# High and low parts of two weight matrices stored interleaved by element, and the SBUF buffers laid out anew

## The chip, the cores and the metric

One core of one Trainium2 chip. The metric is the device time of one launch in microseconds; the number for the kernel before is 1211.54 us, the median of three runs (1210.9 to 1212.32). Engines are named as in the profile: PE is TensorE's matmul side, PEld its weight loads, DVE is VectorE, ACT is ScalarE, POOL is GpSimd, SP is SyncE.

## The reference

A layer of linear attention followed by a gated feed-forward part, gated once more by a ternary product. x is 8 x 2048 x 256 in float32.

```python
xn = layernorm(x)
q, k, v = split(xn @ Wqkv + bqkv)              # 256 -> 3 x 256
qp, kp = elu(q) + 1, elu(k) + 1
kv = einsum('bsd,bse->bde', kp, v)
attn = (qp @ kv) / (qp . sum_s(kp) + 1e-6)
z = layernorm(xn + attn) * g1 + b1
ffn = (silu(z @ Wg + bg) * (z @ Wu + bu)) @ Wd + bd     # 256 -> 682 -> 256
s = layernorm(z + ffn) * g2 + b2
g = silu(xn @ ternary(weight).T * scale)
out = x + s * g
```

## The kernel before, in words

The 16384 rows are worked in 32 groups (`GROUPS`) of 512 rows (`TOK`, four tiles of 128); four groups make one batch. Every exact product is made of three products of rounded parts: `parts3` pairs high with high, low with high and high with low, where the high part is a rounded copy (`f32r`) and the low part the rest. In `products` (L1271) each pair is one weight load (PEld) and one matmul (PE). The left of a pair is the stationary operand, which the weight load brings into the array (128 columns); the right is the moving operand, streamed past it. The load of the next product's stationary operand starts a few ns after the matmul of the present one and runs beside it.

The jobs of TensorE, written out by hand in `TENSOR_JOBS`, are for each group:

- G 0 to 4, U 0 to 4 and GU 5 (`gate_or_up`): 11 jobs of 6 products, stationary a 128 column slice of `wgu_h` or `wgu_l`, moving `zT_h` or `zT_l`, 512 columns. 2112 products in all.
- Q 0 and 1: 6 products each, stationary `wq_h` or `wq_l`, moving `xT_h` or `xT_l`, 512 columns. 384 products.
- D 0 to 5 (`Dn`): stationary `h_h` or `h_l`, moving `wd_h` or `wd_l`, 256 columns; 12 products for each of D 0 to 4, 4 for D 5. 2048 products.
- K, B, XK, KV and N: products with 256 or 258 moving columns, stationary `xT`, `xn`, `kv` (as `xk`) and `qp`.

The steady order of the jobs is

```python
TENSOR_JOBS = steps("""
    K 0, D 4, KV 0, KV 1, D 5, K 1, N 0, N 1, N 2, N 3, G 0, U 0, G 1, U 1, G 2, B 0, U 2, Q 0, Q 1,
    B 1, G 3, D 0, D 1, U 3, G 4, XK 0, U 4, XK 1, XK 2, XK 3, GU 5, D 2, TZ 0, TZ 1, D 3""")
```

so of the eleven gate-up jobs six come right behind a job with 256 or 258 moving columns: G 0 (behind N 3), U 2 (behind B 0), G 3 (behind B 1), U 3 (behind D 1), U 4 (behind XK 0) and GU 5 (behind XK 3). The other five follow a gate-up job.

The weights are split into high and low once, in the fill: `gu_high` (L695 for ACT) writes `wgu_h[:, c, :]`, `setup_gu_low` (L1226 on DVE) writes `wgu_l[:, c, :]`; `setup_q_high` and `setup_qk_low` (L1184) do the same for the query weights. Nothing writes them later.

SBUF buffers are laid out in the order in which `build_kernel` declares them, each at the next multiple of 32 bytes in every partition. All slices of the stationary and moving operands that the six products of a job use are a multiple of 256 bytes from their buffer's start (except for the second half of `qp` and `kv`, which are 32 bytes further), so a buffer's start modulo 256 holds for each of its products:

| buffers | role | before | after |
|---|---|---|---|
| `wgu_h`, `wgu_l` | stationary of G, U, GU | 96 | 224 (high), 228 (low) |
| `zT_h`, `zT_l` | moving of G, U, GU | 96 | 96 |
| `wq_h`, `wq_l` | stationary of Q | 96 | 32 (high), 36 (low) |
| `xT_h`, `xT_l` | moving of Q, stationary of K, B | 96 | 96 |
| `h_h`, `h_l` / `wd_h`, `wd_l` | stationary / moving of D | 96 / 32 | 96 / 32 |
| `wk`, `tern` | moving of K, B | 64 | 64 |
| `xn_h`, `xn_l` / `kp_h`, `kp_l` | stationary / moving of XK | 96 / 0 | 96 / 0 |
| `qp` / `kv` | stationary / moving of N | 96 / 32 | 96 / 32 |
| `wv_h`, `wv_l` | moving of KV | 96 | 224 |
| `xa`, `xn`, `kp`, `xq`, `rz`, `sg`, `hs` | operands of DVE, ACT, POOL and the DMAs | 192 | 224 |

Of the kernel before, what the change touches and what calls it, by code (L numbers as in the profile page):

```python
# [30 lines left out]
P = 128  # L31
D = 256
DC = D // P
H = 682
HF = H // P
HT = H - HF * P
HC = HF + 1
# [6 lines left out]
TOK = 512  # L44
TILES = TOK // P
# [6 lines left out]
SHIFT = 8  # L52
# [9 lines left out]
LN0 = LEAD + 1  # L62
# [150 lines left out]
def build_kernel(nc, x, wqkv, bqkv, wg, bg, wu, bu, wd, bd, g1, b1, g2, b2, wt, out):  # L213
    f32, f32r = mybir.dt.float32, mybir.dt.float32r
# [9 lines left out]
    with ctx:  # L224
        def sb(name, shape, dt=f32):
            return ctx.enter_context(nc.sbuf_tensor(name, shape, dt))
# [2 lines left out]
            return ctx.enter_context(nc.semaphore(name))  # L229


        ident = sb("ident", [P, P])
        consts = sb("consts", [P, 4])
        masks = sb("masks", [P, 2])
        norm1 = sb("norm1", [P, 2, TILES])
        norm2 = sb("norm2", [P, 2, TILES])
        kp_h = sb("kp_h", [P, TILES, D], f32r)
        kp_l = sb("kp_l", [P, TILES, D], f32r)
        den = sb("den", [P, 2, 2])
        wd_h = sb("wd_h", [P, HC, D], f32r)  # L240
        wd_l = sb("wd_l", [P, HF, D], f32r)
        kv_h = sb("kv_h", [P, DC, D + SHIFT], f32r)
        hb = sb("hb", [P, 2 * HC])
        hb0 = sb("hb0", [P, 2 * HC])
        hb1 = sb("hb1", [P, 2 * HC])
        kv_l = sb("kv_l", [P, DC, D + SHIFT], f32r)
        ve = sb("ve", [P, 3, TILES])
        vecs = sb("vecs", [P, 5, DC])
        rstd0 = sb("rstd0", [P, LN0, TILES])
        wk_h = sb("wk_h", [P, DC, D], f32r)  # L250
        wk_l = sb("wk_l", [P, DC, D], f32r)
        tern = sb("tern", [P, DC, D], f32r)
        tscale = sb("tscale", [P, 4])
        wq_h = sb("wq_h", [P, DC, D], f32r)
        wq_l = sb("wq_l", [P, DC, D], f32r)
        xT_h = sb("xT_h", [P, XT, DC, TOK], f32r)
        xT_l = sb("xT_l", [P, XT, DC, TOK], f32r)
        h_h = sb("h_h", [P, HRING, TOK], f32r)
# [3 lines left out]
        zT_l = sb("zT_l", [P, DC, TOK], f32r)  # L262
        xn_h = sb("xn_h", [P, TILES, D], f32r)
        xn_l = sb("xn_l", [P, TILES, D], f32r)
        wv_h = sb("wv_h", [P, DC, D], f32r)
        wv_l = sb("wv_l", [P, DC, D], f32r)
        NGU = (2 * HF + 1) * P
        wgu_h = sb("wgu_h", [P, DC, NGU], f32r)
        wgu_l = sb("wgu_l", [P, DC, NGU], f32r)
        qp_h = sb("qp_h", [P, DC, TOK + SHIFT], f32r)  # L270
        nmr0 = sb("nmr0", [P, LN0, TILES])
        mv = sb("mv", [P, 3, TILES, 2])
        qp_l = sb("qp_l", [P, DC, TOK + SHIFT], f32r)
        st = sb("st", [P, 3, TILES, 6])
        bvb = sb("bvb", [P, D])
        bk1b = sb("bk1b", [P, D])
        g1b = sb("g1b", [P, D])
# [10 lines left out]
        sg = sb("sg", [P, SG, TILES, D])  # L288
        hs = sb("hs", [P, 2, TOK])
        ones, one_zero, neg_half = consts[:, 0:1], consts[:, 1:3], consts[:, 3:4]  # L290
        bq, bq1, nbq, g1c, b1c = (vecs[:, n, :] for n in range(5))
        less_h, less_w = masks[:, 0:1], masks[:, 1:2]
        rstd1, nmr1 = norm1[:, 0, :], norm1[:, 1, :]
# [85 lines left out]

        bias_line = xq[:, 1:3, :, :].rearrange("p a t d -> p (a t d)")[0:1, 0:NGU]  # L380
        b1w = nc.dram_tensor("b1w", (NGU,), f32, kind="Internal").ap()
        turned = nc.dram_tensor("turned", (2, D, TOK), f32, kind="Internal").ap()
        z_turned = nc.dram_tensor("z_turned", (2, D, TOK), f32, kind="Internal").ap()
        ROW_PARTS = [slice(at, min(at + 512, NGU)) for at in range(0, NGU, 512)]

# [3 lines left out]
        xk_h, xk_l = kv_h[:, :, 0:D], kv_l[:, :, 0:D]  # L389
        raw_v = xq[:, 1:3, :, :].rearrange("p a t d -> p (a t d)")[:, NGU:NGU + DC * D].rearrange("p (c n) -> p c n", c=DC)  # L390

# [1088 lines left out]
```

## Time and profile before

| | |
|---|---|
| median of three runs | 1211.54 us (1210.9 to 1212.32) |
| profiled execution, its own time | 1212.66 us |
| its span, first to last instruction | 1211.0 us |
| PE busy | 1190.9 us, 98% |
| PEld busy | 1070.2 us, 88% |
| DVE busy | 1082.2 us, 89% |
| ACT busy | 953.3 us, 79% |
| POOL busy | 841.7 us, 70% |
| mean granted TensorE clock | 0.998 of full speed |

The profiled execution's own time is 1.7 us above its span and 1.1 us above the median of the three runs. A matmul's duration in the rows is longer than its turn on the engine: successive matmuls overlap, since the next one enters while the last one drains. The time from one matmul's start to the next one's start is what each costs; the durations differ from it by a constant.

### The profile page before, as it was taken

How to read it: one execution, taken by the hardware profiler on the slowest of the kernel's cores; microseconds unless marked ns; L12 is line 12 of the kernel's file. 1: busy time of each engine (PE TensorE's matmuls, PEld its weight loads, DVE VectorE, ACT ScalarE, POOL GpSimd, SP SyncE). 2: the span in 40 equal slices, each digit the busy share in tenths (PEclk: the TensorE clock that was granted, in tenths of full speed). 3: DMA queues.
4: the chain of work that ended last, by engine and by line, in shares of the span. 5: the costliest groups of instructions: out<-in, count | busy, mean ns of one | idle time of the engine just before them, and what ended most of it. 6: DMA issues, size and time to landing. Idle time of an engine off the chain costs nothing.

```text
span 1211.0 us, 24021 instructions
## 1 busy us (share of the span) xinstructions
PE 1190.9 (98%) x7550; PEld 1070.2 (88%) x7550; DVE 1082.2 (89%) x2467; ACT 953.3 (79%) x1557; POOL 841.7 (70%) x994
## 2 busy tenths in 40 slices
PE   8999999999999999999999999999999999999997
PEld 6889998989988999989999988999988899888886
DVE  6988999999999999999999999999999999777765
ACT  7787888878888887888878888778797788867753
POOL 3443787767787776787767777667776677766676
PEclk9999999999999999999999999999999999999999
DMA  7213432334432334432234432234332343222201
GB/s 217 74 50 88 123 106 70 88 105 123 123 104 72 87 106 123 118 103 78 87 106 122 121 104 74 74 120 123 108 96 63 101 123 105 70 71 61 76 22 35
DMA packets 137524, 115.61 MB, mean 95 GB/s; under 512 B 12340, under 2 KB 122294, under 8 KB 137399
## 3 DMA queue, kind: packets, MB, share of 16 engines
q1 hardware_dynamic: 137398, 114.08, 32.2%
q8 instruction: 62, 1.02, 0.3%
q14 instruction: 64, 0.52, 0.1%
HBM read 67.38 MB, written 46.67 MB: 94 GB/s over the span
## 4 chain that ended last, share of the span: by engine, by line
PE 86%; DVE 7%; issue 2%; ACT 2%; DMA 1%; POOL 1%; SPq 0%; DVEq 0%; POOLq 0%; ACTq 0%
PE bank L1271 61%; PE d_bank L1271 17%; PE xk_bank L1271 7%; DVE st L922 1%; DMA z_turned<-xa 1%; DMA xa<-z_turned 1%; DVE rz L1054 1%; PE bank L1285 1%; DVE bank L1095 0%; DVE h_l L1105 0%; ACT rz L695 0%; DVE zT_l L1085 0%; POOL norm L569 0%; ACT hs L695 0%; DVE kp L1014 0%
## 5 line engine op out<-in xcount | busy, mean ns | idle before, releaser
L1271 PE MATMUL bank<-zT_h,wgu_h 128*128 128x512 f32 x704 | 275.6, 391 | 1.1 <-DVE rz L1054 1.0
L1271 PE MATMUL bank<-zT_l,wgu_h 128*128 128x512 f32 x704 | 275.7, 392 | 0.0
L1271 PE MATMUL bank<-zT_h,wgu_l 128*128 128x512 f32 x704 | 275.4, 391 | 0.0
L695 ACT ACTIVATE rz<-rz,norm 128x256 f32<-128x256 f32 x252 | 140.5, 596 | 57.7 <-DVE norm L1131 57.1
L569 POOL TENSOR_TENSOR norm<-ve,consts 128x4 f32<-128x4 f32 x64 | 72.9, 1139 | 153.6 <-DVE ve L933 153.5
L1271 PE MATMUL d_bank<-wd_h,h_h 128*128 128x256 f32 x640 | 179.2, 280 | 0.1
L1271 PE MATMUL d_bank<-wd_h,h_l 128*128 128x256 f32 x640 | 179.0, 280 | 0.0
L1271 PE MATMUL d_bank<-wd_l,h_h 128*128 128x256 f32 x640 | 179.0, 280 | 0.0
L1095 DVE SCALAR_TENSOR_TENSOR bank<-bank,hb,hs 128x512 f32<-128x512 f32 x160 | 117.9, 754 | 54.0 <-ACT hs L695 42.3
L695 ACT ACTIVATE h_h<-bank 128x512 fp32r<-128x512 f32 x160 | 95.8, 599 | 80.9 <-DVE bank L1095 80.5
L1271 PEld LDWEIGHTS bank<-zT_l,wgu_h 128*128 128x128 f32 x704 | 132.1, 188 | 28.8
L1271 PEld LDWEIGHTS bank<-zT_h,wgu_h 128*128 128x128 f32 x704 | 132.7, 189 | 25.8 <-DVE rz L1054 3.3
L695 ACT ACT_TABLE_LOAD x116 | 148.8, 1283 | 4.1 <-POOL wd_l L678 1.2
L1271 PEld LDWEIGHTS bank<-zT_h,wgu_l 128*128 128x128 f32 x704 | 132.2, 188 | 20.6
L695 ACT ACTIVATE hs<-bank,hb 128x512 f32<-128x512 f32 x192 | 128.3, 685 | 15.0 <-PE bank L1271 13.6
L592 POOL TENSOR_TENSOR ksum<-ksum,kp 128x256 f32<-128x256 f32 x120 | 106.9, 891 | 46.7 <-DVE kp L1021 43.3
L1105 DVE TENSOR_TENSOR h_l<-bank,h_h 128x512 fp32r<-128x512 f32 x160 | 110.0, 688 | 23.1 <-ACT h_h L695 17.4
L1271 PEld LDWEIGHTS d_bank<-wd_h,h_h 128*128 128x128 f32 x640 | 120.2, 188 | 3.1 <-DVE h_l L1105 0.5
L1271 PEld LDWEIGHTS d_bank<-wd_h,h_l 128*128 128x128 f32 x640 | 120.2, 188 | 2.7
L1271 PEld LDWEIGHTS d_bank<-wd_l,h_h 128*128 128x128 f32 x640 | 122.0, 191 | 0.0
L642 POOL TENSOR_TENSOR rz<-rz,g1b 128x256 f32<-128x256 f32 x128 | 118.0, 932 | 0.0
L602 POOL TENSOR_TENSOR rz<-rz,g2b 128x256 f32<-128x256 f32 x124 | 90.4, 739 | 35.0 <-ACT rz L695 35.0
(163 smaller groups left out, 3576.3 us busy)
## 6 DMA issues: line engine op xcount, KB each, us to landing
xq<-in_L_attn_x_dram SPq DMA_DIRECT2D x32, 512.0 KB, 6.0
xa<-in_L_attn_x_dram SPq DMA_DIRECT2D x31, 512.0 KB, 3.9
out_dram<-rz SPq DMA_DIRECT2D x31, 512.0 KB, 5.0
z_turned<-xa SPq DMA_DIRECT2D x120, 128.0 KB, 3.3
xa<-z_turned SPq DMA_DIRECT2D x30, 512.0 KB, 4.1
turned<-xa SPq DMA_DIRECT2D x108, 128.0 KB, 2.5
xa<-turned SPq DMA_DIRECT2D x27, 512.0 KB, 3.9
rz<-in_L_attn_Wg_dram SPq DMA_DIRECT2D x1, 640.0 KB, 5.2
```

What stands on the lines that cost most here:

```text
L569: eng.tensor_tensor(dst, ve[:, k, :], neg_half[:, 0:1].to_broadcast([P, TILES]), ALU.pow).then_inc(S[f"rs{k}"], 1)
L592: eng.tensor_tensor(ksum[:, slot, :], ksum[:, slot, :], part, ALU.add).then_inc(S["ks"], 1)
L602: eng.tensor_tensor(row_, row_, g2b[:, :], ALU.mult).then_inc(S["a"], 1)
L642: eng.tensor_tensor(row_, row_, g1b[:, :], ALU.mult).then_inc(S["zg"], 1)
L695: return eng.activation(out_, in_, func, **kw).then_inc(S[name], 1)
L922: eng.bn_stats(st[:, k, t, :], rows).then_inc(S[f"bn{k}"], 1)
L1054: eng.scalar_tensor_tensor(out=rz[:, g % RZ, t, :], in0=num[:, 0:D], scalar=den[:, n % 2, 1:2], in1=rz[:, g % RZ, t, :], op0=ALU.mult, op1 ...
L1095: eng.scalar_tensor_tensor(out=hidden(g, c)[0:rows, :], in0=up, scalar=hb[0:rows, HC + c:HC + c + 1], in1=hs[0:rows, n % 2, :], op0=ALU.ad ...
L1105: eng.tensor_tensor(h_l[:, slot, :], hidden(g, c)[:, :], h_h[:, slot, :].bitcast(f32), ALU.subtract).then_inc(S["hl"], 1)
L1271: ins = eng.matmul(dst, left, right, start=first and n == 0, stop=last and n == len(pairs) - 1, **kw)
L1285: ins = eng.transpose(dst[:, c * D + t * P:c * D + (t + 1) * P], src[:, 2 * p + t, c * P:(c + 1) * P], ident[:, :])
```

## The change

The high and the low part of the gate-up weights become one buffer `wgu` with the parts side by side: element n of the high part is followed by element n of the low part, so that a slice of 128 columns of either part is read with a step of 8 bytes, over 1024 bytes instead of 512. The same for the query weights (`wq`). The names `wgu_h`, `wgu_l`, `wq_h` and `wq_l` remain as views, so all code that uses them is unchanged. The declarations are put in another order, with one spare buffer of 32 bytes, which gives the starts in the column "after" of the table above. No instruction is added, removed or moved on any engine. In a trace the four views have the names `wgu` and `wq`, and lines behind the declarations stand one further down.

```diff
-        ident = sb("ident", [P, P])
+        NGU = (2 * HF + 1) * P
+        rstd0 = sb("rstd0", [P, LN0, TILES])
+        wgu = sb("wgu", [P, DC, NGU, 2], f32r)
         consts = sb("consts", [P, 4])
...
-        wq_h = sb("wq_h", [P, DC, D], f32r)
-        wq_l = sb("wq_l", [P, DC, D], f32r)
+        norm2 = sb("norm2", [P, 2, TILES])
...
+        spare0 = sb("spare0", [P, 8])
+        ident = sb("ident", [P, P])
         wv_h = sb("wv_h", [P, DC, D], f32r)
         wv_l = sb("wv_l", [P, DC, D], f32r)
-        NGU = (2 * HF + 1) * P
-        wgu_h = sb("wgu_h", [P, DC, NGU], f32r)
-        wgu_l = sb("wgu_l", [P, DC, NGU], f32r)
...
         ones, one_zero, neg_half = consts[:, 0:1], consts[:, 1:3], consts[:, 3:4]
+        wgu_h, wgu_l = wgu[:, :, :, 0], wgu[:, :, :, 1]
+        wq_h, wq_l = wq[:, :, :, 0], wq[:, :, :, 1]
```

where `wq = sb("wq", [P, DC, D, 2], f32r)` now stands between `wd_l` and `norm1`.

## Rows read from the trace of the kernel before

**Rows 1.** The page, part 1: busy time of each engine, share of the span, instructions.
```profile
PE 1190.9 (98%) x7550; PEld 1070.2 (88%) x7550; DVE 1082.2 (89%) x2467; ACT 953.3 (79%) x1557; POOL 841.7 (70%) x994
```
**Rows 2.** Groups of PE, shapes apart: busy us, mean ns; idle before, releaser.
```profile
L1271 PE MATMUL bank<-zT_l,wgu_h 128*128 128x512 f32 x704 | 275.7, 392 | 0.0
L1271 PE MATMUL bank<-zT_h,wgu_h 128*128 128x512 f32 x704 | 275.6, 391 | 1.1 <-DVE rz L1054 1.0
L1271 PE MATMUL bank<-zT_h,wgu_l 128*128 128x512 f32 x704 | 275.4, 391 | 0.0
L1271 PE MATMUL d_bank<-wd_h,h_h 128*128 128x256 f32 x640 | 179.2, 280 | 0.1
...
L1271 PE MATMUL bank<-xT_h,wq_h 128*128 128x512 f32 x128 | 51.5, 402 | 0.0
L1271 PE MATMUL bank<-xT_h,wq_l 128*128 128x512 f32 x128 | 50.1, 391 | 0.0
L1271 PE MATMUL bank<-xT_l,wq_h 128*128 128x512 f32 x128 | 50.0, 391 | 0.0
```
**Rows 3.** Timeline of PE, 18 gate-up products in a row, first and last: start, duration us.
```profile
627.61 0.39 PE L1271 MATMUL bank<-zT_h,wgu_h 128*128 128x512 f32 x1
...
631.69 0.28 PE L1271 MATMUL bank<-tern,xT_h 128*128 128x256 f32 x1
```
**Rows 4.** Tile wgu_h, 627.6 to 631.4 us: duration ns min/median/max.
```profile
L1271 PE MATMUL bank<-zT_h,wgu_h x6: 389/389/389, 627.6 to 631.0; 128*128 128x512 f32 x6
```
**Rows 5.** Tile wgu_h, 600.0 to 601.1 us, right behind a B job.
```profile
L1271 PE MATMUL bank<-zT_l,wgu_h x2: 397/397/397, 600.3 to 601.0; 128*128 128x512 f32 x2
```
**Rows 6.** Tile wgu_h, 607.4 to 608.7 us, right behind an XK job.
```profile
L1271 PE MATMUL bank<-zT_h,wgu_h x2: 393/395/397, 607.4 to 608.1; 128*128 128x512 f32 x2
```
**Rows 7.** Timeline of PE, three query products around a wait.
```profile
635.18 0.39 PE L1271 MATMUL bank<-xT_l,wq_h 128*128 128x512 f32 x1
635.49 0.50 PE L1271 MATMUL bank<-xT_h,wq_h 128*128 128x512 f32 x1
635.83 0.39 PE L1271 MATMUL bank<-xT_h,wq_l 128*128 128x512 f32 x1
```
**Rows 8.** Timeline of PEld in the same stretch.
```profile
634.96 0.19 PEld L1271 LDWEIGHTS bank<-xT_l,wq_h 128*128 128x128 f32 x1
635.49 0.19 PEld L1271 LDWEIGHTS bank<-xT_h,wq_h 128*128 128x128 f32 x1 [0.34 <-DVE h_l L1105]
635.60 0.19 PEld L1271 LDWEIGHTS bank<-xT_h,wq_l 128*128 128x128 f32 x1
```
**Rows 9.** Tile wd_h, 602.0 to 603.9 us and 612.4 to 615.0 us.
```profile
L1271 PE MATMUL d_bank<-wd_h,h_h x6: 276/276/276, 601.9 to 603.6; 128*128 128x256 f32 x6
L1271 PE MATMUL d_bank<-wd_h,h_h x8: 281/281/281, 612.3 to 614.8; 128*128 128x256 f32 x8
```
**Rows 10.** Timeline of PE, D 2 and D 3 (24 products) and their neighbours.
```profile
612.09 0.39 PE L1271 MATMUL bank<-zT_l,wgu_h 128*128 128x512 f32 x1
612.32 0.28 PE L1271 MATMUL d_bank<-wd_h,h_h 128*128 128x256 f32 x1
...
615.15 0.28 PE L1271 MATMUL bank<-wk_h,xT_h 128*128 128x256 f32 x1
```
**Rows 11.** Tiles wgu_h and wgu_l: the writes in the fill, and the readers.
```profile
L695 ACT ACTIVATE wgu_h<-rz,vecs x2: 1452/1454/1455, 26.1 to 29.2; 128x1408 fp32r<-128x1408 f32 x2
L1226 DVE SCALAR_TENSOR_TENSOR wgu_l<-rz,vecs,wgu_h x2: 1679/1681/1683, 27.6 to 33.7; 128x1408 fp32r<-128x1408 f32 x2
L1271 PE MATMUL bank<-zT_h,wgu_l x704: 387/389/398, 78.1 to 1197.8; 128*128 128x512 f32 x176
```

More of the change, by code:

```diff
@@ L229, in sem @@
             return ctx.enter_context(nc.semaphore(name))
-        ident = sb("ident", [P, P])
+        NGU = (2 * HF + 1) * P
+        rstd0 = sb("rstd0", [P, LN0, TILES])
+        wgu = sb("wgu", [P, DC, NGU, 2], f32r)
         consts = sb("consts", [P, 4])
-        masks = sb("masks", [P, 2])
-        norm1 = sb("norm1", [P, 2, TILES])
-        norm2 = sb("norm2", [P, 2, TILES])
         kp_h = sb("kp_h", [P, TILES, D], f32r)
         kp_l = sb("kp_l", [P, TILES, D], f32r)
-        den = sb("den", [P, 2, 2])
+        masks = sb("masks", [P, 2])
         wd_h = sb("wd_h", [P, HC, D], f32r)
         wd_l = sb("wd_l", [P, HF, D], f32r)
[L242 to L249, printed above, removed]
+        wq = sb("wq", [P, DC, D, 2], f32r)
+        norm1 = sb("norm1", [P, 2, TILES])
         wk_h = sb("wk_h", [P, DC, D], f32r)
@@ L252, in build_kernel @@
         tern = sb("tern", [P, DC, D], f32r)
-        tscale = sb("tscale", [P, 4])
-        wq_h = sb("wq_h", [P, DC, D], f32r)
-        wq_l = sb("wq_l", [P, DC, D], f32r)
+        norm2 = sb("norm2", [P, 2, TILES])
         xT_h = sb("xT_h", [P, XT, DC, TOK], f32r)
@@ L264, in build_kernel @@
         xn_l = sb("xn_l", [P, TILES, D], f32r)
+        qp_h = sb("qp_h", [P, DC, TOK + SHIFT], f32r)
+        den = sb("den", [P, 2, 2])
+        nmr0 = sb("nmr0", [P, LN0, TILES])
+        kv_l = sb("kv_l", [P, DC, D + SHIFT], f32r)
+        qp_l = sb("qp_l", [P, DC, TOK + SHIFT], f32r)
+        hb = sb("hb", [P, 2 * HC])
+        hb0 = sb("hb0", [P, 2 * HC])
+        kv_h = sb("kv_h", [P, DC, D + SHIFT], f32r)
+        hb1 = sb("hb1", [P, 2 * HC])
+        ve = sb("ve", [P, 3, TILES])
+        vecs = sb("vecs", [P, 5, DC])
+        tscale = sb("tscale", [P, 4])
+        mv = sb("mv", [P, 3, TILES, 2])
+        st = sb("st", [P, 3, TILES, 6])
+        spare0 = sb("spare0", [P, 8])
+        ident = sb("ident", [P, P])
         wv_h = sb("wv_h", [P, DC, D], f32r)
         wv_l = sb("wv_l", [P, DC, D], f32r)
-        NGU = (2 * HF + 1) * P
-        wgu_h = sb("wgu_h", [P, DC, NGU], f32r)
-        wgu_l = sb("wgu_l", [P, DC, NGU], f32r)
[L270 to L274, printed above, removed]
         bvb = sb("bvb", [P, D])
```

## The prediction

> **What bounds the kernel now.** The page's first part comes first: PE is busy for 98% of the span, no other engine for over 89% [rows 1]. So the time is the sum of what TensorE's 7550 products take, and only two things can move it: the time from one product's start to the next one's, or a wait of PE. The change moves no instruction, so I look at the products themselves.
>
> The groups of PE show which products the change touches [rows 2]: 2112 gate-up products, whose three rows add up to 275.7 + 275.6 + 275.4 = 826.7 us or 391.4 ns each, and 384 query products, 51.5 + 50.1 + 50.0 = 151.6 us. A duration is not a price, since products overlap. The timeline gives the price: 18 gate-up products in a row start from 627.61 to 631.69 us, 226.7 ns apart [rows 3], and in that stretch each has a duration of 389 ns, minimum, median and maximum [rows 4]. So 389 ns of duration stand for 226.7 ns of time, and each ns above it is a ns of time. Behind a B job the same product has 397 ns [rows 5], behind an XK job 393 to 397 ns [rows 6]. Same instruction, same shape, same granted clock (0.998 over the whole span), nothing waits: what differs is how the weight load beside it falls in time against the moving stream. I read the surplus as the two reads of SBUF by TensorE getting in each other's way, and call 389 ns the clean state.
>
> Is 389 ns itself a state with collisions? The query product at 635.18 us has no load beside it: the one before began at 634.96 and the next at 635.49, behind a wait [rows 8]. It too has 0.39 us [rows 7]. So the clean state is the floor of the moving stream, with nothing in it for a new layout of the weights. The same rows price a load: where product and load start together, the next load follows after 635.60 - 635.49 = 0.11 us, and the product's duration is 0.50 instead of 0.39 us. A load with 128 columns occupies its side for about 110 ns: half of a 512 column product's 226.7 ns, but nearly all of a 256 column product's turn.
>
> D shows what a bad phase costs there: its products have 276 ns at 602 to 604 us and 281 ns at 612 to 615 us [rows 9]; 24 of the latter take 615.15 - 612.32 = 2.83 us, 117.9 ns each [rows 10]. The good stretch came behind gate-up products of 397 ns [rows 5], the bad one behind clean ones. The states hang together: what a job inherits decides how it runs.
>
> **The change, part by part.**
>
> *Gate-up.* The load of 128 columns now steps by 8 bytes and goes over 1024 bytes. If it keeps its rate (110 ns), its address moves by 1024 / 110 = 9.3 bytes per ns; the moving stream's by 2048 / 226.7 = 9.0. Before, the load went at 4.7, so the stream overtook it, and whether they met on the way hung on the phase. Now they go almost in step, and the distance at the start (128 bytes modulo 256) stays: over a whole load it drifts by (9.3 - 9.0) x 110 = 33 bytes. If what collides is set by the address modulo 256, or by a smaller power of two that 128 is not a multiple of, they never meet, whatever the phase. Then all gate-up products are clean: 826.7 - 2112 x 0.389 = 5.1 us gone. The ends: nothing gained (0), and at worst all products in the worst state of the rows, 397 ns: 2112 x 0.397 - 826.7 = +11.8 us. I take -5.1, since the two rates match so well and the distance is the largest there is.
>
> *Query.* Of 151.6 - 384 x 0.389 = 2.2 us surplus, 128 x (402 - 389) = 1.7 us belong to each job's first product, which starts together with its load behind a wait [rows 2, 7]; a layout doesn't touch that. I take the rest, -0.5 us. The distance is only 64 bytes; at worst 384 x (397 - 391) = +2.3 us.
>
> *What D inherits.* The clean stretches of D stood behind dirty gate-up products. With clean ones throughout, D 0 and D 1 lose them: all 1920 products at 281 ns are 539.5 us against 179.2 x 3 = 537.6 us (the three D groups are alike, one is shown) [rows 2, 9]: +1.9 us. The other end is that D comes out clean instead, 1920 x (280 - 276) = -7.7 us; nothing in the rows makes that likely, since the loads and operands of D keep their distance of 64 bytes. I take +1.9 us. K, B, XK and N keep all distances, too; I cost them at nothing.
>
> *The fill.* ACT writes the high part in 2 x 1.45 us and DVE the low part in 2 x 1.68 us [rows 11], now with a step of 8 bytes. No row shows an 8-byte step, so the price lies between nothing and twice: at most 2 x 1.68 = +3.4 us, if the two DVE writes doubled and all of it were on PE's path. ACT's write works off 128 x 1408 elements at 1.03 ns each, with its operand from SBUF; I take 0, because G 0, the first reader, comes at 78 us, long behind the last write at 33.7 us [rows 11], and what is delayed in between are single steps beside PE's own queue.
>
> *The other buffers.* Operands of DVE, ACT, POOL and the DMAs shift from 192 to 224 modulo 256. PE has 98%; none of these engines is waited for enough to matter, so 0.
>
> **Sum:** -5.1 - 0.5 + 1.9 = -3.7 us. Against the profiled execution's 1212.66 us that is 1208.96 us; this execution stood 1.1 us above the median of 1211.54 us, so the median should come out at 1207.8 us, 0.3% less. A measurement of this kernel can tell about 0.2% (2.4 us) from no change, so the forecast is just beyond that.
>
> **The rivals.**
>
> *Nothing happens.* The surplus of the dirty states has another cause, or is made elsewhere as fast as it is removed (D at 281 ns is one such place). For it: the gain that can be had is small, 5.6 us, and a phase decides it, not an address that the rows vary; only D's +1.9 us is needed once more to fall under 0.2%. Time: 1211.5 us, from 1209.2 to 1213.9. The Trainium skill, "TensorE: Matmul & The Clock Gate", Part 2, and "SBUF — State Buffer", "Who interferes with whom", say that the weight load has a read port of its own, so that loading the next weights takes nothing from the running matmul. By that rule there is nothing to gain and the change is worth 0; the trace speaks against it in that one product has 389 or 397 ns with nothing but a load beside it.
>
> *In step, and colliding (slower).* What makes the two reads meet never also makes them meet always, if the phase at the start adds the missing bytes: the load starts a few ns behind its matmul, and a few ns are some tens of bytes at 9 bytes per ns. If what counts is the address modulo 128 or 64, a distance of 128 or 64 is none. Also, a load now touches twice as many lines of whatever width. Place: every gate-up and query product. Price: with products at 395 ns on average, the middle of the dirty rows [rows 6], 2112 x (395 - 391.4) = +7.6 us: 1219.1 us. It decides from about 392.5 ns on, where 2.4 us are lost.
>
> *The load becomes slower with its step (slower, more).* A gate-up job's first load runs beside a product with 256 columns, which gives it only some 118 ns [rows 10]. Six jobs per group stand so, 6 x 32 = 192. A load of 1.5 x 110 = 165 ns adds 47 ns each, +9.0 us: 1220.6 us; of twice the time +102 ns each, +19.6 us: 1231.1 us. No row shows a load with a step. The Trainium skill, "SBUF — State Buffer", "SBUF cachelines", wants at least two hits in a line of 16 bytes for full bandwidth; a step of 8 bytes gives just two, so by that page this rival falls. No row here shows it.
>
> *The floor falls.* Were the 226.7 ns themselves collisions, 2496 products could gain. The Trainium skill, "TensorE: Matmul & The Clock Gate", Part 1, gives 215.7 ns between matmuls with 512 columns; by it, up to 11 x 2496 = 27.5 us would go. From the rows alone: 512 columns at the granted 2.4 GHz take 213.3 ns, 13.4 ns less than 226.7, so at most 33 us. Against it stands the product with no load beside it and the same 0.39 us [rows 7, 8].
>
> **How the numbers follow.** Forecast (gate-up clean, D worse or as before): 0.49. Nothing happens: 0.25. In step and colliding: 0.16. Slower load: 0.07. Floor falls: 0.03. Nearly all of the forecast is faster by over 0.2%, a little of it is not, and the floor adds its share: faster 0.50. Same 0.26, slower 0.24. The forecast's own range is 1205.0 (both gains, D as before: -5.6, and 0.9 for jobs that come out cleaner) to 1209.2. The range asked to hold the time 8 times in 10 goes on over "nothing happens" to the colliding case's middle: 1205.0 to 1218.0. It leaves out the slower load, the floor and the upper half of the colliding case.
>
> **What would show it.** In the profile after: the gate-up groups at 389 ns mean instead of 391 and 392, with 389 also behind XK and B jobs (right), or at 393 and more everywhere (the colliding rival). The 18 products between N 3 and B 0 still 226.7 ns apart (floor), and the D groups at 281 (my +1.9) or below 280 (wrong, in the kernel's favour). A slower load shows as a PEld mean above 188 ns and as a longer gap in front of U 2, G 3, U 3, U 4 and GU 5. ACT L695 and DVE L1227 on `wgu` above 1.45 and 1.68 us show a price in the fill. Wrong altogether would be a change in K, XK, N or B, whose operands keep their distances.

## The result, and the profile after

The changed kernel takes 1216.0 us (median of 5 runs, 1215.22 to 1217.15) against 1212.06 us (median of 5) for the kernel before: ratio 1.0036, 95% interval 1.0023 to 1.005. It is slower by 4.4 us by the ratio (the two medians are 3.9 us apart), where 1207.8 us, a gain of 3.7 us, was forecast. The time lies in the range (1205.0 to 1218.0), on the side of the rival "in step, and colliding": it does so because the range reached over to that rival, not by the forecast's own mechanism.

Busy time by engine, changed kernel, answering to [rows 1]:

```profile
PE 1196.2 (98%) x7550; PEld 1089.6 (90%) x7550; DVE 1080.9 (89%) x2467; ACT 953.6 (78%) x1557; POOL 842.4 (69%) x994
```

TensorE has all of it: PE +5.3 us and the weight loads +19.4 us, while DVE has 1.3 us less and ACT and POOL stay within 0.7 us. Groups of PE and PEld, shapes apart, changed kernel (busy us, mean ns), answering to [rows 2]; the first group's busy time is that of products which overlap, so only its mean is of use:

```profile
L1272 PE MATMUL bank<-zT_h,wgu 128*128 128x512 f32 x1408 | 440.9, 394 | 0.8 <-DVE rz L1055 0.8
L1272 PE MATMUL bank<-zT_l,wgu 128*128 128x512 f32 x704 | 277.0, 393 | 0.0
L1272 PE MATMUL d_bank<-wd_h,h_h 128*128 128x256 f32 x640 | 179.1, 280 | 0.0
...
L1272 PE MATMUL bank<-xT_l,wq 128*128 128x512 f32 x128 | 50.4, 394 | 0.0
...
L1272 PEld LDWEIGHTS bank<-zT_h,wgu 128*128 128x128 f32 x1408 | 261.0, 196 | 39.5 <-DVE rz L1055 2.3
```

The gate-up products have 393 to 394 ns instead of 391.4. Their loads have 196 ns; the kernel before has

```profile
L1271 PEld LDWEIGHTS bank<-zT_h,wgu_h 128*128 128x128 f32 x704 | 132.7, 189 | 25.8 <-DVE rz L1054 3.3
```

and 188 ns for the two other groups. D is where it was. In the stretch between N 3 and B 0, where the kernel before was clean, the timeline of PE now reads (x2: two products merged):

```profile
629.99 0.62 PE L1272 MATMUL bank<-zT_h,wgu 128*128 128x512 f32 x2
...
634.61 0.39 PE L1272 MATMUL bank<-zT_l,wgu 128*128 128x512 f32 x1
634.85 0.28 PE L1272 MATMUL bank<-tern,xT_h 128*128 128x256 f32 x1
```

and the tile's durations there

```profile
L1272 PE MATMUL bank<-zT_h,wgu x14: 391/393/397, 629.5 to 634.2; 128*128 128x512 f32 x14
```

21 products from 629.99 to 634.85 us are 231.4 ns each, against 226.7 ns [rows 3] and 389/389/389 [rows 4]. Not one product of this stretch is clean. Compare that with the forecast: all clean. Over the whole trace, 63% of the gate-up products have a duration of at most 389 ns in the kernel before, up to 27 of them in a row; in the changed one 3% have it, and never two in a row.

A lone load tells more. Where product and load start together behind a wait, two loads of the changed kernel read

```profile
1128.75 0.31 PEld L1272 LDWEIGHTS bank<-zT_h,wgu 128*128 128x128 f32 x2 [1.21 <-DVE rz L1055]
```

The two starts are 115 ns apart; in the kernel before, at the same place,

```profile
1124.83 0.19 PEld L1271 LDWEIGHTS bank<-zT_h,wgu_h 128*128 128x128 f32 x1 [1.42 <-DVE rz L1054]
1124.94 0.19 PEld L1271 LDWEIGHTS bank<-zT_h,wgu_l 128*128 128x128 f32 x1
```

they are 108 ns apart. The load itself is 7 ns longer with its 8-byte step, and its product's stream hardly runs beside it, since it has to wait for the load. All pairs of gate-up loads whose first one comes behind a pause of over 150 ns agree: 9 in the kernel before are 108 to 109 ns apart, 7 in the changed one 115 to 119 ns.

**The measure used from here on.** For each product the time from its start to the next one's, less 226.7 ns (512 columns) or 113.3 ns for 256 columns (the same per column; it is also what D's clean products take, [rows 9]), summed over a trace; products more than 25 ns above that are waits and stand apart. I call the sum the surplus. The kernel before has 4.8 us for the gate-up products, 0.8 for Q, 6.3 for D and 15.6 for all others, 27.5 in all; the changed one 10.9, 2.4, 6.1 and 15.4, in all 34.7: +7.2 us. Waits take 2.8 us of it back (41.1 us before, 38.3 after). But that part can't be put down to the change: the profiled runs of all kernels below except e4 lie between 37 and 42 us, the one of before among the highest, so a surplus can't be turned into a time to better than 1 to 3 us. What stands in a trace is therefore used to say where, and the ratio to say how much.

### The profile page after: what moved, and what is told of

Read it like the earlier page. It is cut to its first block, busy times and chain, and to the rows that moved or that the text cites. A ratio compares the mean times of both kernels' runs of the same rounds, so it can differ in the third digit from the quotient of the medians.

```text
span 1215.4 us, 24021 instructions
## 1 busy us (share of the span) xinstructions
PE 1196.2 (98%) x7550; PEld 1089.6 (90%) x7550; DVE 1080.9 (89%) x2467; ACT 953.6 (78%) x1557; POOL 842.4 (69%) x994
## 4 chain that ended last, share of the span: by engine, by line
PE 81%; DVE 9%; ACT 4%; issue 4%; DMA 1%; POOL 1%; SPq 0%; DVEq 0%; ACTq 0%; POOLq 0%
PE bank L1272 57%; PE d_bank L1272 16%; PE xk_bank L1272 7%; DVE st L923 1%; ACT rz L696 1%; DVE bank L1096 1%; DVE rz L1055 1%; DVE h_l L1106 1%; DMA xa<-z_turned 1%; DMA z_turned<-xa 1%; DVE zT_l L1086 1%; PE bank L1286 1%; ACT hs L696 1%; POOL norm L570 1%; ACT h_h L696 0%
## 5 line engine op out<-in xcount | busy, mean ns | idle before, releaser
L1272 PE MATMUL bank<-zT_h,wgu 128*128 128x512 f32 x1408 | 440.9, 394 | 0.8 <-DVE rz L1055 0.8
L1272 PEld LDWEIGHTS bank<-zT_h,wgu 128*128 128x128 f32 x1408 | 261.0, 196 | 39.5 <-DVE rz L1055 2.3
L1272 PE MATMUL bank<-zT_l,wgu 128*128 128x512 f32 x704 | 277.0, 393 | 0.0
L1272 PEld LDWEIGHTS bank<-zT_l,wgu 128*128 128x128 f32 x704 | 137.9, 196 | 25.3
L656 POOL CAST ht<-hs 32x512 fp32r<-32x512 f32 x63 | 51.4, 815 | 82.0 <-DVE hs L1096 75.0
L616 POOL TENSOR_TENSOR rz<-rz,sg 128x256 f32<-128x256 f32 x124 | 103.9, 838 | 5.0
```

The costliest lines, as they stand in the source:

```text
L616: eng.tensor_tensor(row_, row_, sg[:, g % SG, t, :], ALU.mult).then_inc(S["c"], 1)
L656: eng.tensor_copy(ht[n * MAIN:(n + 1) * MAIN, :], hs[0:MAIN, (HC * g + HF) % 2, :]).then_inc(S["ha"], 1)
L1272: ins = eng.matmul(dst, left, right, start=first and n == 0, stop=last and n == len(pairs) - 1, **kw)
```

## The experiments

After the result: theory STEP, the 8-byte step itself costs; PLACE (later DISTANCE), the new distance costs; OTHERS, the shifted operands of the other engines do. Each kernel was timed beside the kernel before, whose median was 1209.85, 1211.2, 1210.42 and 1210.68 us in the four sets (e1 to e4, e5 to e8, e9 to e12, e13 to e15).

**e1_gu_step** and **e3_q_step**: the step without the move.

```diff
 # e1, in the kernel before
-        wgu_h = sb("wgu_h", [P, DC, NGU], f32r)
-        wgu_l = sb("wgu_l", [P, DC, NGU], f32r)
+        wgu = sb("wgu", [P, DC, NGU, 2], f32r)
...
+        wgu_h, wgu_l = wgu[:, :, :, 0], wgu[:, :, :, 1]
 # e3, in the kernel before
-        wq_h = sb("wq_h", [P, DC, D], f32r)
-        wq_l = sb("wq_l", [P, DC, D], f32r)
+        wq = sb("wq", [P, DC, D, 2], f32r)
...
+        wq_h, wq_l = wq[:, :, :, 0], wq[:, :, :, 1]
```

> The layout of before with one edit: the gate-up weights interleaved at the place where they stood (residue 96, distance 0 from zT), the query weights as before. Theory STEP (the 8-byte step itself costs, wherever the buffer stands: in the changed kernel a load behind a wait, with nothing beside it, is followed by the next one after 115 ns instead of 108): slower than before by 4 to 6 us, about 1217 us, weight loads at 195 to 196 ns mean, gate-up products at 393 to 394 ns. Theory PLACE (what costs is the new distance of 128 bytes, not the step): same as before within 1 us, products 391 ns. Theory OTHERS (the shifted operands of the other engines cost it): same as before, too.

> The layout of before, only the query weights interleaved at their place (residue 96, distance 0). 384 products against 2112: STEP: a surplus of 4 ns each, +1.5 us at most, about 1213 us, loads of wq at 195 ns. PLACE and OTHERS: no change, below 0.5 us.

e1: 1214.44 us, ratio 1.0039 (1.0026 to 1.0051). e3: 1212.24 us, 1.0021 (1.0012 to 1.0031). Both as STEP has it, e3 (+2.5 us by the ratio) even above its +1.5 us. The loads of e1 have 193 and 194 ns, a little under the 195 to 196 expected. Groups of e1, PE:

```profile
L1271 PE MATMUL bank<-zT_l,wgu 128*128 128x512 f32 x704 | 277.5, 394 | 0.0
L1271 PE MATMUL d_bank<-wd_h,h_h 128*128 128x256 f32 x640 | 177.7, 278 | 0.0
```

and of e3:

```profile
L1271 PE MATMUL d_bank<-wd_h,h_h 128*128 128x256 f32 x640 | 180.0, 281 | 0.1
L1271 PE MATMUL bank<-xT_h,wq 128*128 128x512 f32 x256 | 81.5, 399 | 0.0
```

Nothing of D was touched in either, and D moves in both: its surplus goes from 6.3 to 2.1 us in e1, and to 8.4 us in e3. In e1, what D inherits (-4.2 us) is half as large as what the step costs the gate-up products (+8.6 us).

**e2_after_plain**: the move without the step; the reverse of both diffs above in the changed kernel.

> The layout of the changed kernel, every buffer at its new place, but high and low parts of both weights stored one after the other again (distances 128 and 64, step 4 bytes). STEP: back to the time of before, 1211 to 1213 us, loads at 188 ns, gate-up products at 391 ns or below. PLACE: stays at 1216 us with products at 393 to 394 ns and loads at 188. OTHERS: stays at 1216 us with products at 391 ns and longer waits of PE.

1215.12 us, ratio 1.0044 (1.0032 to 1.0057): PLACE, in full, though e1 had just given it to STEP. Loads at 188 ns, products at 394 to 395 ns:

```profile
L1272 PE MATMUL bank<-zT_h,wgu_h 128*128 128x512 f32 x704 | 277.8, 395 | 0.2 <-DVE rz L1055 0.2
L1272 PE MATMUL bank<-zT_l,wgu_h 128*128 128x512 f32 x704 | 277.4, 394 | 0.0
```

So either half of the change costs about as much by itself as the whole change (the step was tried on gate-up and query weights one at a time, not on both together). The theories don't exclude each other; the next runs take distance alone, and both for the gate-up part alone.

**e4_gu_step16**: `wgu = sb("wgu", [P, NGU, DC, 2], f32r)` in the kernel before, so that a load steps by 16 bytes.

> The layout of before, gate-up weights interleaved four ways (high and low of both halves of the contraction side by side), so that a load steps by 16 bytes over 2048 bytes. STEP, if the price goes by the bytes spanned: a lone load goes from 108 ns (4 bytes) and 115 ns (8 bytes) to some 130 ns (three times the surplus, 7 x 3 = 21), and the 192 gate-up jobs' starts behind 256-column products cost 15 ns more each; all in all +10 to +15 us, 1222 to 1227 us. STEP, if it is a price for any step: as e1. PLACE and OTHERS: as before.

1241.75 us, ratio 1.0263 (1.0249 to 1.0277), twice as much as the highest value expected. Loads and products of e4, and its lone load:

```profile
L1271 PEld LDWEIGHTS bank<-zT_l,wgu 128*128 128x128 f32 x704 | 218.9, 311 | 0.0
L1271 PE MATMUL bank<-zT_h,wgu 128*128 128x512 f32 x1408 | 466.8, 413 | 0.4 <-DVE rz L1054 0.4
```
```profile
1151.82 0.54 PEld L1271 LDWEIGHTS bank<-zT_h,wgu 128*128 128x128 f32 x2 [0.76 <-DVE rz L1054]
```

The two starts are 213 ns apart. It is the only such pair in e4. So a load of 128 columns takes 108, 115 and 213 ns at a step of 4, 8 and 16 bytes: nearly free, then double. 213 ns fit under a product of 512 columns (226.7 ns), not under one of 256. The gate-up products above the 25 ns line, 182 of 187 of them right behind a job with 256 or 258 columns, sum to 22.7 us against 2.1 before, +20.6 us, and the gate-up surplus rises from 4.8 to 16.1 us, +11.3 us. Together that is 31.9 us, the difference of the medians; the fit to 0.1 us is chance, since other products move, too (D -1.4 us) and the spans of the two profiled executions are 29.2 us apart. The Trainium skill, "SBUF — State Buffer", "SBUF cachelines", wants at least two accesses to a line of 16 bytes for full bandwidth. Two of four bytes each are there at a step of 8, one at 16, and the loads show the cliff where the Trainium skill puts it, though the step of 8 still costs 7 ns.

**e5_gu_128** and **e7_gu_step_128**: the gate-up buffers alone, moved ahead of `norm2` in the kernel before (residue 224); in e7 interleaved. **e6_others**: only the other engines' operands.

```diff
 # e5 (in e7: wgu = sb("wgu", [P, DC, NGU, 2], f32r) and the two views)
+        NGU = (2 * HF + 1) * P
+        wgu_h = sb("wgu_h", [P, DC, NGU], f32r)
+        wgu_l = sb("wgu_l", [P, DC, NGU], f32r)
         norm2 = sb("norm2", [P, 2, TILES])
 # e6
+        spare0 = sb("spare0", [P, 8])
         bvb = sb("bvb", [P, D])
```

> The kernel before with one edit: the two gate-up buffers, contiguous as they are, declared ahead of norm2, which puts them at residue 224 (distance 128 from zT) and moves no other buffer's residue. Theory DISTANCE (the place of the gate-up weights relative to zT is by itself enough for the cost of the changed layout with plain weights, 1.0044): +4 to +5.5 us, ratio 1.0035 to 1.0045, weight loads unchanged at 188 ns, gate-up products at 393 to 394 ns, D a little better than before. Theory OTHERS (the cost there came from the query weights' place or from the other engines' operands): ratio 1.000, products at 391 ns.

> The kernel before with a spare buffer of 32 bytes ahead of bvb: the operands of DVE, ACT, POOL and the DMAs go from 192 to 224 modulo 256, all of TensorE's steady operands stay. DISTANCE: no difference, within 0.1%, groups of PE with the same means. OTHERS: up to the whole +4 to +5 us.

> As e5_gu_128 (distance 128), but the gate-up weights interleaved, so the change's gate-up part alone. If step and distance add up: e1's 1.0039 and e5's some 1.004 give 1.008. If they don't, because each only takes away the clean state which the other one takes away too: ratio 1.002 to 1.004, gate-up surplus near the changed kernel's 10.9 us in all, below the 13.4 us which the interleaved weights have at distance 0.

e5: 1214.93 us, 1.0033 (1.002 to 1.0046). e6: 1210.42 us, 0.9998 (0.999 to 1.0007). e7: 1216.37 us, 1.0043 (1.0031 to 1.0055). OTHERS is out. Moving the gate-up weights alone costs 4 us, and with the step on top the price hardly grows: step and distance don't add. In e5:

```profile
L1271 PE MATMUL bank<-zT_l,wgu_h 128*128 128x512 f32 x704 | 277.4, 394 | 0.0
```

**e8_d_0**: `wd_h`, `wd_l` declared ahead of `wv_h` in the kernel before, at D's distance 0.

> The kernel before with wd_h and wd_l moved to residue 96, so that D, too, has a distance of 0 between stationary and moving operand (64 before). If distance 0 is what lets a contiguous load and the moving stream fall into a clean state, D's 1920 products go from 280 ns towards 276 ns and up to 6 us are gained (ratio 0.995). If each shape has its own best distance, D goes to 281 ns or above: +2 us or more.

1215.49 us, 1.0038 (1.0026 to 1.005), the other way. D's surplus goes from 6.3 to 11.8 us:

```profile
L1271 PE MATMUL d_bank<-wd_l,h_h 128*128 128x256 f32 x640 | 181.0, 283 | 0.0
L1271 PEld LDWEIGHTS d_bank<-wd_l,h_h 128*128 128x128 f32 x640 | 122.4, 191 | 0.0
```

Distance 0, where the gate-up weights of the kernel before stand, is worse than 64 for D's 256 columns.

**e11_gu_64, e12_gu_step_64, e14_gu_step_192, e15_gu_192**: as e5 and e7, at the other two 64-byte places, ahead of `masks` (residue 160) and of `wd_h` (residue 32).

> The kernel before with the contiguous gate-up weights at residue 160, distance 64 from zT, where e5_gu_128 had 128 and before 0. If only distance 0 has a clean state for 512 columns: as e5, ratio 1.003 to 1.004, gate-up surplus about 11 us. If the surplus grows with the distance: half of that, ratio about 1.0015 to 1.002, surplus about 8 us.

> As e11, with interleaved gate-up weights. Interleaved they had a surplus of 13.4 us at distance 0 and 10.7 to 10.9 us at 128. My mechanism of the prediction (load and stream in step, a start distance that keeps them apart) wants some distance at which the surplus falls below the 4.8 us of before: if 64 is that one, ratio below 1.000. If a load with an 8-byte step has no clean state at any distance: surplus 10 to 14 us, ratio 1.003 to 1.005.

> The last 64-byte place for interleaved gate-up weights: residue 32, distance 192 (or -64) from zT. 0, 64 and 128 gave a gate-up surplus of 13.4, 8.9 and 10.7 us. STEP (no distance gives a load with an 8-byte step a clean state): 8 to 14 us, ratio 1.002 to 1.005. The mechanism of the prediction (some start distance keeps load and stream apart): below 4.8 us, ratio at most 1.000.

> The same place for contiguous gate-up weights. 0, 64 and 128 gave 4.8, 13.8 and 11.3 us. If distance 0 alone has the clean state: 9 to 14 us, ratio 1.003 to 1.005. If a place ahead of the moving stream is as good as the same line: below 6 us, ratio 1.000 to 1.001.

| distance from zT | contiguous: gate-up surplus, ratio | 8-byte step: gate-up surplus, ratio |
|---|---|---|
| 0 | 4.8 us, 1 (before) | 13.4 us, 1.0039 (e1) |
| 64 | 13.8 us, 1.0056 (1.0042 to 1.0069) (e11) | 8.9 us, 1.0030 (1.0019 to 1.0041) (e12) |
| 128 | 11.3 us, 1.0033 (e5) | 10.7 us, 1.0043 (e7) |
| 192 | 6.9 us, 1.0029 (1.0018 to 1.004) (e15) | 14.3 us, 1.0056 (1.0042 to 1.007) (e14) |

With the step no place comes near the 4.8 us of before: STEP for e12 and e14, though 8.9 us at 64 and 14.3 at 192 lie just outside what STEP had, so the distance matters there as well. Contiguous, the surplus depends on the distance as strongly, and 0 is best. Neither alternative had the size at 64, where e11 came out above e5, nor at 192, where e15's 6.9 us fall between the two. What was lost is a lasting state more than an average: at 192 contiguous 27% of the gate-up products have at most 389 ns, in the six other forms 6% or fewer, and none of the seven has more than two such products in a row. At 64 bytes the step even beats the contiguous form (its surplus 8.9 against 13.8 us, ratio 1.0030 against 1.0056), at 128 they are alike. e15's ratio (+3.5 us) is more than its surplus explains (+1.1 us in all). The two profiled executions are only 1.7 us apart (1214.37 against 1212.66 us), because that of before stood 2.0 us above the median of this set; so most of the rest lies in the trace of before, not in e15.

One thing the moves share: e5, e7, e11, e12, e14 and e15 all bring the gate-up weights from behind `zT` to the front of SBUF, some 100000 bytes away, and no run puts them there at distance 0. That 64 bytes matter is shown at the front: e5 and e11 differ in that and in the places of two small buffers, `masks` and `norm1` (surplus 11.3 and 13.8 us, ratios 1.0033 and 1.0056, whose intervals just overlap). That a far move by a whole multiple of 256 bytes does nothing shows in other products, with 256 or 258 columns: in e5 `kv` moves 22528 bytes against `qp`, and the surplus of N goes from 5.1 to 5.0 us; in e15 `xn` moves as far against `kp`, and that of XK goes from 3.6 to 3.7 us. For the gate-up products themselves it is not shown.

**e9_kb_64, e10_xk_64, e13_kb_xk_64**: `wk_h`, `wk_l`, `tern` (e9), `kp_h`, `kp_l` (e10) or all five (e13) declared ahead of `wd_h` in the kernel before, at D's distance of 64.

> The kernel before with wk_h, wk_l and tern moved from residue 64 to 32, so that K and B (256 moving columns) have the distance of 64 between stationary and moving operand that D has, 32 before. D shows products without surplus at 64, K and B none at 32 (surplus 4.9 ns each on 1280 products, 6.2 us in all). If 64 is the good distance for 256 columns: K and B go to D's 3.3 ns or less, -2 to -4 us, ratio 0.997 to 0.998. If what a job inherits decides: no change, or a new pattern of either sign, up to 2 us.

> The same for XK: kp_h and kp_l from residue 0 to 32, distance from xn 96 before, 64 now. 672 products with a surplus of 5.4 ns. If 64 is good for 256 columns: -1.4 to -2.5 us, ratio 0.998 to 0.999; else no change within 1 us.

> Both moves of e9 and e10 in the kernel before: moving operands of K, B and XK at residue 32, 64 bytes from their stationary operands. The profiles of e9 and e10 had a surplus of all products of 25.1 and 25.6 us against 27.5 before. If the savings add: 23 to 24 us and a ratio of 0.9965 to 0.998. If the jobs behind inherit other states (each alone came out at 0.9990 and 0.9998 in time): 0.998 to 1.000.

e9: 1209.38 us, 0.9990 (0.9980 to 0.9999). e10: 1210.38 us, 0.9998 (0.9989 to 1.0007). e13: 1210.13 us, 0.9993 (0.9984 to 1.0002). In the traces the surplus falls as hoped, from 27.5 to 25.1, 25.6 and 23.9 us; e10 does it less in XK itself (3.6 to 2.9 us) than in the gate-up jobs behind it (4.8 to 3.7 us). In time nearly nothing arrives. e9 beats both kernels by 0.1%, just beyond its interval; e13 can't be told from before. That the saving is given back in waits was not shown: one profile of each is too few for waits that differ by 4 us between profiles.

## Why the prediction was wrong

*What bounds the kernel, the clean state, the price per ns of duration:* right. The time came from TensorE alone, in the products named. The mean duration of the gate-up products rose by 2.5 ns, 5.3 us over 2112 of them, and their turns by 5.5 us (surplus +6.1, waits -0.6). No layout has gate-up products clearly below 226.7 ns, so the rival of the falling floor is out.

*The gate-up term, -5.1 us:* this step failed. It said that load and stream go in step, so that a distance of 128 bytes at the start keeps them apart and every gate-up product comes out clean. The measured surplus went up from 4.8 to 10.9 us, +6.1, in the half of the bounds (0 to +11.8) that I had not taken. Two things stand against the argument. The load didn't keep its rate: 115 ns instead of 108 for a lone one. And there is no distance in steps of 64 bytes at which the interleaved form is clean (the table), which it would have to have if a start apart meant a way apart. The argument took the clean state of before as one in which collisions happen to be few. It is more than that: at distance 0 contiguous loads settle into it and stay, for 18 products in a row [rows 3]. The change gave that up twice, by the step and by the move, and each by itself is enough: 1.0039 and 1.0033 for the gate-up part alone, 1.0043 for both. What the two reads do to each other in detail is not shown by any run; that they collide at certain addresses remains a reading.

*The query term, -0.5 us:* wrong in the same way; surplus +1.6 us (0.8 to 2.4), inside the bound of +2.3. e3, with the step at distance 0, has a query surplus of 2.3 us, too. The query products' waits fell from 2.4 to 0.8 us in the same two profiles, so how much of it reached the time is not shown; e3 as a whole cost 1.0021.

*D inherits, +1.9 us:* right that D depends on the gate-up jobs ahead of it, with the sign shown by e1 and e3: where gate-up lost its clean state, D won 4.2 us, and where its surplus fell from 4.8 to 3.5 us (e3), D lost 2.1 us, about the +1.9 forecast for that case. In the changed kernel the gate-up jobs were not clean, so the premise fell, and D came out at -0.2 us. It is a term that can't be worked out from a row of one layout: e1 and e7 have the same step and D surpluses of 2.1 and 7.5 us.

*The fill and the other buffers, 0:* right. The DVE writes took 1678 and 1687 ns as before, the ACT writes 1563 and 1621 instead of 1454 ns, and only DVE waited for one of them, 1.1 us in both kernels; e6 puts the shift of the other engines' operands at 0.9998.

*The rivals.* "In step, and colliding" is what happened as to place and sign, with 393.9 instead of 395 ns. Its reason, that being in step makes it worse, is only half of it, since the contiguous form, which by the prediction's rates isn't in step, does the same at 64 and 128. "The load becomes slower" is true by 7 ns instead of 55, which is too little to be seen in front of the six jobs; with 16 bytes it holds in full, +20.6 us against the 19.6 worked out for a load of twice the time. "Nothing happens" is out by the ratio, and every other form of the gate-up weights that was tried cost time as well. The Trainium skill, "TensorE: Matmul & The Clock Gate", Part 2, gives the load a read port of its own that takes nothing from a running matmul. e5 changes no residue but that of the loaded buffer, and the products beside the loads take 394 instead of 391 ns: small, but not nothing.

Still open is the rule behind the table: why 0, then 192, are good for contiguous loads beside 512 columns, 64 better than 0 beside 256, and what about a start decides. Distances that are no multiple of 64 were not tried for the gate-up weights, nor distance 0 at another place in SBUF.

## What to carry to other kernels

- On a kernel at 98% of PE, look at the distribution of one product's duration, not at its mean: a run of equal minimum values is a locked good state, worth knowing before a layout is touched. Another place for a stationary buffer, 64 to 192 bytes from its moving operand modulo 256, cost 0.3 to 0.6% here.
- Keep stationary operands contiguous, unless a run says otherwise (at distance 64 the step of 8 bytes was the better form). A step of 8 bytes costs 7 ns a load, and no tried place had the locked state with it; a step of 16 bytes doubles the load, which then shows behind every product with 256 columns.
- A layout is judged by the whole time, and by one edit at a time: neighbours whose code and addresses stay the same moved by 4.2 us down (D in e1) and 2.1 us up (D in e3).

## What the runs showed of the hardware that I had not expected

- A weight load and the matmul beside it are coupled by the addresses of their operands: the 512-column product costs 226.7 ns at best and 229 to 233 ns on average, by where the loaded buffer stands (contiguous, at four places modulo 256).
- The state is handed on between products of different jobs and shapes: D had 276 or 281 ns, and which of the two goes with the last gate-up product before it. Of the 66 stretches of D right behind a gate-up job in the kernel before, 42 of the 43 behind a last product of 388 or 389 ns take 117.7 or 117.8 ns a product, all 23 behind one of 397 or 398 ns take 114.0 or 114.1. In e3, 65 of 66 are of the first kind; in e1, 65 of 66 stand behind a last product of 395 ns and take 113.6 to 114.2. In e1 its median was 276 ns, in the kernel before 281:

```profile
L1271 PE MATMUL d_bank<-wd_h,h_h x640: 276/276/388, 92.1 to 1202.8; 128*128 128x256 f32 x160
```
```profile
L1271 PE MATMUL d_bank<-wd_h,h_h x640: 276/281/384, 92.1 to 1201.0; 128*128 128x256 f32 x160
```

- A load of 128 columns takes 108, 115 and 213 ns at steps of 4, 8 and 16 bytes.
